# Eight fp32 transposes of an expert tile, each set behind a first-layer product

## What is computed

```
def _L0_ffn_ref(x, router_w, w1, v1, w2, bias):
    D = 256; F = 704; E = 8; TOP_K = 2
    xt = x.reshape(B * S, d)
    scores = jax.nn.softmax(xt @ router_w, axis=-1)
    expert_weights, expert_idx = jax.lax.top_k(scores, TOP_K)
    h = gelu(einsum('td,edf->tef', xt, w1)) * einsum('td,edf->tef', xt, v1)
    y = einsum('tef,efd->ted', h, w2)
    yk = jnp.take_along_axis(y, expert_idx[:, :, None], axis=1)
    out = jnp.sum(expert_weights[:, :, None] * yk, axis=1) + bias
```

## Time and profile before

| | us |
|---|---|
| median of 3 executions | 955.04 (954.33 to 958.66) |
| the profiled execution | 956.73 |
| its span, first to last instruction | 955.0 |
| PE busy | 837.5 (88% of the span) |
| DVE busy | 622.6 (65%) |
| POOL busy | 443.8 (46%) |
| ACT busy | 363.2 (38%) |
| expert stage | 444 to 955 |

### The profile page before, as it was taken

The page is one execution under the profiler, slowest core; times in us unless marked ns, Lnnn a source line. Parts: engine busy times, 40 slices in busy tenths (PEclk is TensorE's granted clock), DMA queues, the critical chain, the costliest instruction groups (busy, mean ns, idle before and its releaser), DMA issues.

```text
span 955.0 us, 20303 instructions
## 1 busy us (share of the span) xinstructions
PE 837.5 (88%) x5017; PEld 744.2 (78%) x5018; DVE 622.6 (65%) x1688; ACT 363.2 (38%) x658; POOL 443.8 (46%) x438
## 2 busy tenths in 40 slices
PE   5558899988989989523999999999999999999994
PEld 2447888877878978522898998989989899899994
DVE  3775798878888677462556556565565756655653
ACT  2736465546455342221224224242242423322221
POOL 1434364756658566573234434344343434433333
PEclk9869999989999979755999999999999999999997
DMA  7000402202010220446122424325242121212221
GB/s 266 23 23 1 138 23 68 90 24 89 28 61 34 79 68 35 157 154 213 30 43 37 127 45 117 55 34 134 38 127 45 34 45 34 44 34 44 34 45 16
DMA packets 48928, 65.22 MB, mean 68 GB/s; under 512 B 4928, under 2 KB 43968, under 8 KB 48896
## 3 DMA queue, kind: packets, MB, share of 16 engines
q1 hardware_dynamic: 30704, 41.83, 14.9%
q0 software_dynamic: 13392, 18.27, 9.6%
q10 hardware_dynamic: 4800, 4.74, 1.5%
HBM read 41.28 MB, written 23.54 MB: 68 GB/s over the span
## 4 chain that ended last, share of the span: by engine, by line
PE 63%; POOL 9%; DVE 9%; issue 7%; ACT 6%; DMA 3%; ACTq 0%; DVEq 0%; SPq 0%; POOLq 0%
PE ps L1309 13%; PE ps L1311 13%; PE ps L1310 13%; PE ps L1342 5%; PE ps L454 4%; PE ps L455 4%; PE ps L456 4%; POOL routed L1169 3%; POOL hid_lo L369 3%; ACT squares L652 2%; PE ps L1318 2%; DMA out_rows<-y_moe,tok_moe 1%; DVE h_sb L884 1%; ACT xn_sb L668 1%; DVE stats L863 1%
## 5 line engine op out<-in xcount | busy, mean ns | idle before, releaser
L1309 PE MATMUL ps<-w_moe_hi,xT_moe_hi 128*128 x426 | 167.4, 393 | 1.3 <-DVE xT_moe_lo L1441 1.3
L1495 POOL TENSOR_TENSOR y_moe<-y_moe 128x256 f32<-128x256 f32 x71 | 51.8, 729 | 240.4 <-DVE y_moe L1459 240.4
L1311 PE MATMUL ps<-w_moe_lo,xT_moe_hi 128*128 x426 | 161.4, 379 | 0.0
L1310 PE MATMUL ps<-w_moe_hi,xT_moe_lo 128*128 x426 | 161.2, 378 | 0.0
L1501 POOL DMA_INDIRECT out_rows<-y_moe,tok_moe x71 | 111.0, 1564 | 33.2 <-issue 32.8
L1400 ACT ACTIVATE hidT_hi<-ps 128x768 fp32r<-128x768 f32 x71 | 57.7, 812 | 163.6 <-PE ps L1342 163.6
L1309 PE MATMUL ps<-w_moe_hi,hidT_hi 128*128 x355 | 106.6, 300 | 2.3 <-issue 2.3
L1394 ACT ACTIVATE gelu_moe<-ps 128x704 f32<-128x704 f32 x71 | 53.8, 758 | 133.8 <-PE ps L1311 133.8
L1311 PE MATMUL ps<-w_moe_lo,hidT_hi 128*128 x355 | 101.0, 284 | 0.0
L1310 PE MATMUL ps<-w_moe_hi,hidT_lo 128*128 x355 | 100.5, 283 | 0.0
L1459 DVE SCALAR_TENSOR_TENSOR y_moe<-ps,gate_moe,gates 128x256 f32<-128x256 f32 x142 | 62.1, 479 | 52.6 <-PE ps L1357 46.6
(11 more groups left out here) (197 smaller groups left out, 2035.1 us busy)
## 6 DMA issues: line engine op xcount, KB each, us to landing
raw<-in_w SPq DMA_DIRECT2D x8, 1408.0 KB
x_moe<-routed SPq DMA_DIRECT2D x74, 132.5 KB, 2.3
raw<-in_w SPq DMA_DIRECT2D x8, 640.0 KB
x_sb<-in_x SPq DMA_DIRECT2D x8, 512.0 KB, 4.4
x_again<-in_x SPq DMA_DIRECT2D x8, 512.0 KB, 3.7
out_rows<-x_again ACTq DMA_DIRECT2D x8, 512.0 KB
wmod_sb<-in_wmod SPq DMA_DIRECT2D x1, 1536.0 KB, 6.6
gu_raw<-in_gu_t SPq DMA_DIRECT2D x1, 1536.0 KB, 13.2
```

The source lines that it names most:

```text
L1309: pe.matmul(dst, a_hi, b_hi, start=first, stop=False)
L1310: pe.matmul(dst, a_lo, b_hi, start=False, stop=False)
L1311: return pe.matmul(dst, a_hi, b_lo, start=False, stop=last)
```

## The change

`x_transposes` and `hid_transposes` become functions for a single transpose. `first_products` gets a function `beside` that it calls after each of its 18 products, numbered 0 to 17. After products 1 to 6 it issues one transpose of `hid_moe` of tile t-1, and after products 9 and 10 one transpose of `x_moe` of tile t+1. The same instructions are issued as before, with the same semaphores. The programs of the other engines are the same.

```
-            def x_transposes(t):
-                pe.wait_ge(rows_in[t.slot], t.round * 16 + 16)
-                if t.n >= 1:
-                    pe.wait_ge(xT_l, t.v)
-                for k in range(KD):
-                    mm = pe.transpose(xT_ps[:, k * P:(k + 1) * P], x_moe[:, t.slot, k * P:(k + 1) * P], ident)
-                mm.then_inc(xT_t, 1)
+            def x_transpose(t, k):
+                if k == 0:
+                    pe.wait_ge(rows_in[t.slot], t.round * 16 + 16)
+                    if t.n >= 1:
+                        pe.wait_ge(xT_l, t.v)
+                mm = pe.transpose(xT_ps[:, k * P:(k + 1) * P], x_moe[:, t.slot, k * P:(k + 1) * P], ident)
+                if k == KD - 1:
+                    mm.then_inc(xT_t, 1)
...
+                        pe.matmul(y, x_hi, w_moe_hi[:, w], start=(k == 0), stop=False)
+                        beside(n * 6 + k * 3)
+                        pe.matmul(y, x_lo, w_moe_hi[:, w], start=False, stop=False)
+                        beside(n * 6 + k * 3 + 1)
+                        mm = pe.matmul(y, x_hi, w_moe_lo[:, w], start=False, stop=(k == KD - 1))
+                        if n >= 1 and k == KD - 1:
+                            mm.then_inc((a_mm, b_mm)[n - 1], 1)
+                        beside(n * 6 + k * 3 + 2)
...
+            HID_FROM, X_FROM = 1, 9
+
+            def transposes_beside(t):
+
+                def beside(n):
+                    if t.n >= 1 and HID_FROM <= n < HID_FROM + KF:
+                        hid_transpose(t.near(-1), n - HID_FROM)
+                    if X_FROM <= n < X_FROM + KD:
+                        x_transpose(t.near(1), n - X_FROM)
+                return beside
...
             def step(t):
                 e = entry(pe, TAB_EXPERT, t, E - 1)
-                hid_transposes(t.near(-1))
-                first_products(t, e)
-                x_transposes(t.near(1))
+                first_products(t, e, transposes_beside(t))
                 second_product(t.near(-1), pe.snap(kept, min_val=0, max_val=E - 1))
                 pe.reg_mov(kept, e)
```

More of the change, by code:

```diff
@@ L1311, in three, with first_products @@
                 return pe.matmul(dst, a_hi, b_lo, start=False, stop=last)
-            def x_transposes(t):
-                pe.wait_ge(rows_in[t.slot], t.round * 16 + 16)
-                if t.n >= 1:
-                    pe.wait_ge(xT_l, t.v)
-                for k in range(KD):
-                    mm = pe.transpose(xT_ps[:, k * P:(k + 1) * P], x_moe[:, t.slot, k * P:(k + 1) * P], ident)
-                mm.then_inc(xT_t, 1)
-            def first_products(t, e):
+            def x_transpose(t, k):
[6 more added lines that the diff above has]
+                    mm.then_inc(xT_t, 1)
+            def first_products(t, e, beside):
                 pe.wait_ge(w13_lo, e + 1)
@@ L1331, in first_products, with hid_transpose @@
                         w = bass.ds((e & 1) * EXPW + (k * 2 * F + lo), hi - lo)
[L1332 to L1343, removed]
+                        x_hi, x_lo, y = xT_moe_hi[:, t.par, k, :], xT_moe_lo[:, t.par, k, :], ps[:, n, 0:hi - lo]
+                        pe.matmul(y, x_hi, w_moe_hi[:, w], start=(k == 0), stop=False)
[6 more added lines that the diff above has]
+                        beside(n * 6 + k * 3 + 2)
+            def hid_transpose(t, k):
+                if k == 0:
+                    pe.wait_ge(hid_r, t.v + 1)
+                    if t.n >= 1:
+                        pe.wait_ge(hidT_l, t.v)
+                mm = pe.transpose(hidT_ps[:, k * P:(k + 1) * P], hid_moe[:, k * P:(k + 1) * P], ident)
+                if k == KF - 1:
+                    mm.then_inc(hidT_t, 1)
+            HID_FROM, X_FROM = 1, 9
[6 more added lines that the diff above has]
+                return beside
             def second_product(t, e):
@@ L1362, in first @@
                 e = entry(pe, TAB_EXPERT, t, E - 1)
-                x_transposes(t)
-                first_products(t, e)
-                x_transposes(t.near(1))
+                for k in range(KD):
+                    x_transpose(t, k)
+                first_products(t, e, transposes_beside(t))
                 pe.reg_mov(kept, e)
@@ L1376, in last @@
             def last(t):
-                hid_transposes(t)
+                for k in range(KF):
+                    hid_transpose(t, k)
                 second_product(t, pe.snap(kept, min_val=0, max_val=E - 1))
```

## The result

| | us |
|---|---|
| median after, 4 executions | 1054.23 (1051.99 to 1057.12) |
| median before, 4 executions | 955.68 (954.33 to 958.66) |
| ratio | 1.103 (95% interval 1.099 to 1.107) |
| the profiled execution after, its span | 1053.81, 1052.0 |

The account below looks back on a forecast made before the run. PE bounds ordinary tiles at 6.77 us before; after, a loop over ACT and DVE does at 7.88. Over 70 tiles that adds 91.8, the clock 7, to 956.73: 1055.5 profiled, forecast 1054, range 1020 to 1090.

Parts of the forecast that it names:

- Rival 3: Transposes cost 0.06 behind a product and the loop doesn't bind: 28 us less, 927; chance 0.03.
- The loop: From PE's first product through the last `hid_moe` transpose, ACT and DVE back to PE: 7.88 us an ordinary tile.
- The slack: Before the change, the sequencer's wait for `b_mm` ahead of `multiply`: 0.35 us in an ordinary tile.
- One sign: PE idle for `xT_l` before nearly every step: about 1.1 us, 65 to 70 times, 80 to 110 us.
- Rival 2: DVE's sequencer reaches the branch and table load ahead of L1437; loop 6.95, +25, 980; chance 0.05.
- The clock: PE's clock falls behind each split's idle time: 1.2 us per split, bounds 0 and 1.7, +7 in all.
- The ends: The first tile and the tail behind the last run of six change by no more than a few tenths.
- Rival 4: The clock falls in ordinary tiles too: 96 us more, 1150, or 1078 if in a quarter of them; chance 0.07.
- The late L1437: The few late ends of `take_gates` on DVE mostly vanish; all four staying on the loop would add up to 6.
- `hidT_l`: Second layer starts at X + 4.9 instead of 4.74 (X: first product streams); PE's 0.2 delay costs nothing.
- the first one: The loop through DVE holds as worked out: 1054, own range 1020 to 1090; chance 0.82.
- The fifth: Nothing measurable: the waits move but all have cover, 955; chance 0.03.

Follow-up runs that it names:

- The run with `x_moe` alone: Kernel after, with the six `hid_moe` transposes back as one run at the head of the step; only the `x_moe` pair stays moved: 958.20, ratio 1.0015.
- the interleaved kernel without waits: Kernel after plus `take_gates` and `xT_rest` moved earlier on DVE, PE's expert read ahead of the second layer, `hid_moe` transposes behind products 0 to 5: 975.77, ratio 1.021.
- the run with a second load: Kernel after, with one more unused load from the table at the end of each DVE step: 1090.40.
- when `xT_l` was made early: Kernel after, with `take_gates` ahead of `hidT_rest` and `xT_rest` ahead of `multiply` on DVE: 1023.36, ratio 1.071.
- two kernels that relieved DVE in the tiles with a split: Kernel before with `take_gates` ahead of `hidT_rest`: 962.27; kernel before with DVE's split cut in halves over two steps: 961.67.

## Why the prediction was right, point by point

- **The transposes cost 0.11 wherever they stand.** In the timeline of the result the last two transposes of `hid_moe` ahead of ACT are 0.345 apart with one product between them, 0.234 + 0.11. The run with `x_moe` alone (+0.4 us in 70 tiles) and the interleaved kernel without waits (6.80 a tile) agree. The Trainium skill (TensorE: Matmul & The Clock Gate, Part 2) says that weight loads are pulled ahead of matmuls in flight. The trace shows the pull (a transpose's load runs beside the product ahead of it), and placing a transpose there still costs 0.11. Whether that is its own streaming or the load of the product behind it, these rows don't separate. Rival 3 falls.
- **The loop, term by term** (forecast, then the tile from 719.95): first streaming product to last transpose 2.18, 2.18; to ACT 0.30, 0.31; to `hidT_rest` 0.85, 0.84; to L1454 1.71, 1.71; to `multiply` 1.04, 1.05; to `xT_rest` and through it 0.94 + 0.42, 0.94 + 0.42. Only the last term was too large: 0.34 + 0.1 for PE's start, of which the chain shows 0.23 of issue time in most tiles, and 0.33 to 0.41 at a turn of PE's own loop. That is most of the 0.10 by which 7.88 was over the 7.78 of this tile; at the median of 7.80 the loop was 0.08 too long, 4 us in 49 tiles.
- **The slack was more than the forecast's sentence says.** It names 0.35, which is the wait at `b_mm`. The whole loop, with the last transpose back at 0.54, would be 7.80 - 1.64 = 6.16, some 0.6 below PE's 6.77. The kernel with `x_moe` alone shows nearly this: 1.58 to 1.60 from L1454 to L1467, where 1.05 would do. The 1.64 minus this 0.6 is the 1.0 that the tile grew by. The forecast's sum didn't use the 0.35, so its total is untouched.
- **One sign missed.** PE was to wait for `xT_l` for 80 to 110 us in all, some 1.1 in a tile; the profile has 65.3, and 0.6 in an ordinary tile. The tile did grow by 1.0. From the last product of the second layer to the first of the next step are 0.91 in place of 0.12; the modelled end of the product before covers 0.16 of that, and 0.12 is the usual distance. The first product then delays the second by 0.10, and 0.13 is lost ahead of the second layer, which waits for `hidT_l`.
- **The load and the branch behind L1454 are serial.** In the loop all ordinary tiles show 1.04 to 1.06 from L1454 to L1467, 1.56 to 1.61 at a turn and 3.61 to 3.63 at a split. The chain through one of these gaps names what is in it (DVEq is DVE's sequencer, L1265 the line of the table load):

```profile
725.09 0.08 DVE tok_moe L1454
725.17 0.14 issue
725.30 0.06 DVEq L1265
725.37 0.03 issue
725.40 0.31 DVEq L1265
725.71 0.03 issue
725.75 0.19 DVEq L1265
725.93 0.03 issue
725.97 0.02 DVEq L1265
725.99 0.05 issue
726.04 0.05 DVEq L1465
726.09 0.04 issue
726.14 0.11 DVE hid_moe L1467
```

  The load itself is 0.31 of 1.05 and register operations behind it 0.19. Rival 2, in which they run ahead of L1454, falls here, and the run with a second load confirms it: 0.64 more in an ordinary tile.
- **The clock was mis-sized, and its upper bound was too low.** The forecast took 1.2 us for each of six splits, with a bound of 1.7. The tiles behind a split took 1.3, 2.1, 1.4, 2.1, 2.1 and 2.1 more than their like, 11.0 in all against 7. The low level lasted longer than the forecast had it, over all seven products and five transposes ahead of the last one and over products behind it; the granted clock is 0.50 or 0.51 in every window from 611 to 617:

```profile
614.00:616.00 2.00, 2.00 (x8) 1.54 (x7) 0.00 (x0) 0.36 (x1) 1.57 (x1) 0.50 0.98 251
617.00:618.00 1.00, 1.00 (x7) 0.88 (x7) 0.92 (x5) 0.29 (x1) 0.00 (x0) 1.00 1.01 412
```

  The 2.18 of this tile became 4.0: seven products at 0.43 and five transposes at 0.21. Here the error of 4 us up happened to meet that of 4 us down in PE's start, so the total is better than its terms, by luck.
- **The ends did change.** The prediction allowed a few tenths for the first tile and the tail. The first `multiply` came 1.0 earlier and the tail was 1.9 shorter, in part since the low level covered fewer of the last tile's products (the last section has its windows). Together with the 1.1 by which the distances came out over the forecast, that leaves the profiled span 1.8 under it.
- **Ordinary gaps left the clock alone.** PE has some 1.0 us to spare in each ordinary tile (7.80 against the 6.80 of its work), and the stretch from 455 to 515 kept 1.00. Rival 4 falls.
- **The late L1437 vanished**, as said: DVE's wait for the scatter, 5.0 in four waits before, has no row after the change. What lies before 444 us is unchanged: PE is busy for 350.1 us there, against 349.8.
- **`hidT_l`.** The prediction said that its delay cost nothing inside a step that ends by waiting for `xT_l`. That held, but by 0.3 only (7.5 against 7.8), and the prediction didn't close that path into a loop through PE's own load from the table. Its price came out when `xT_l` was made early.
- Of the rivals the first one holds. The fifth (the waits have cover) falls, since PE's waits weren't covered.

What isn't settled: how the 14.9 us around the splits of the last interleaved kernel divide between the longer split, the clock behind it and the late scatter. No run takes these apart.

## What to carry to other kernels

Before a step is moved on a busy engine, ask which result of it starts a chain over other engines, and how late the last instruction that makes this result becomes: here six transposes that cost the same in either place moved the end of their group 1.64 us later into the step (2.18 against 0.54), in a loop with some 0.6 us of slack, and each ordinary tile paid the difference of 1.0. Sum that loop term by term, with the sequencers' branches and loads from tables in it as serial work, since whatever hides them is gone as soon as their engine is the late one. And look for the second-longest loop too: cutting the first down by 0.87 brought 0.3, because another one lay just below it.

## What the runs showed of the hardware that wasn't expected

- **PE's sequencer costs when PE is waited for.** A load from the table ahead of a step took 0.58 of each tile (7.51 against 6.93) once PE's queue had no more work in it than the 17 short products behind a wait; before the change the step's transposes followed the second layer after 0.16 (718.02 to 718.18 in its timeline), since PE was the late one and its sequencer was ahead.
- **At the low clock a transpose takes 0.21.** Product and transpose together took 0.64 behind a split (614.54 to 615.18, products of 0.43), twice the 0.345 of an ordinary tile.
- **The same idle time, two outcomes.** Before the change the clock was at its low level within a microsecond of PE's restart behind 2.33 us of idle time (the earlier trace rows and the third line of the earlier trace rows). After the change the last tile has the same idle time ahead of the same products, and the level was still full in the first of these windows and low in the second; the products lengthen from 1040.2 on, 1.4 us after the restart. The chain first, then the windows:

```profile
1036.46 2.33 issue
```

```profile
1039.00:1040.00 1.00, 1.00 (x10) 1.00 (x10) 0.20 (x2) 0.00 (x0) 0.83 (x1) 1.00 0.00 0
1041.00:1042.00 1.00, 0.65 (x4) 0.35 (x2) 0.31 (x1) 0.00 (x0) 0.00 (x0) 0.50 0.51 78
```

  Idle time alone doesn't say when the level falls. In the tiles before it PE had been about 88% busy after the change and fully busy before it; whether that matters wasn't tried.
- **A stall that is taken away can come back as a wait for a transfer.** In two kernels that relieved DVE in the tiles with a split, its late wait for the scatter's completion grew from 5.0 to 9.5 and 11.4 us (four waits each), and both ended slower than the kernel before.
